# A two-layer transformer/state-space kernel: the stage ahead of the scan rebuilt, expert pieces given new places

## The chip, the cores and the metric

The kernel runs on one core of a Trainium2 chip. The core has a matrix engine (PE, with its weight loads shown as PEld), a vector engine (DVE), a scalar engine for activations (ACT), GpSimd (POOL) and a queue engine (SP) that issues most transfers. The metric is the device time of one launch in microseconds (us), median of three runs.

## What is computed

Eight sequences (B = 8) of T = 512 tokens with 128 features pass through two layers. Each layer norm is modulated by a conditioning vector, and each block is gated before it is added to the residual.

```python
# layer 0
x = x + g0 * attention(mod(layernorm(x)))          # 8 heads, latent keys and values, causal softmax
gates = top2_softmax(h @ w_gate.T)                 # 8 experts of 64 hidden units, computed densely
x = x + g1 * sum_e gates[:, e] * (gelu(h @ fc_e) @ proj_e)
# layer 1
x_in, res = split(h @ in_proj_w + b)               # 256 + 256 channels
xc = silu(conv4(x_in) + conv_b)                    # causal, 4 taps
d_raw, Bm, Cm = split(xc @ x_proj_w + b)
delta = softplus(d_raw @ dt_proj_w + dt_proj_b)
for n in range(16):                                # state index; a scan over the 512 tokens
    h[n, t] = exp(delta * A[n]) * h[n, t-1] + delta * xc * Bm[n]
y = sum_n h[n] * Cm[n] + xc * D_skip
x = x + g2 * ((y * silu(res)) @ out_proj_w + b)
x = x + g3 * top2_moe(mod(layernorm(x)))           # 8 experts of 512 hidden units, top 2 of 8
```

The experts of layer 1 are computed sparsely: tokens are sorted by expert into 15 blocks of 128 rows (`NB = 15`), each with the weights of one expert (512 KB).

## The kernel before

**One sequence after another, software-pipelined.** Each engine has a program written out by hand, in order, and engines meet only at semaphores. An iteration `b` goes through four stages: attention of `b` (DVE `attend`, L1542 on); the stage ahead of the scan (layer 0's experts, then in-projection, convolution, x-projection and softplus); the scan; then attention of `b+1` begins. Into this order the layer-1 experts of sequence `b-1` are laid ("behind"), and the projections of `b+1` ("ahead"): `project(b+1, k)` on PE and `take_queries`, `take_keys`, `take_values` on ACT.

**The scan.** There are 16 states and 2 halves of the channels, so 32 scan instructions, k = 2n + c. For each k, ACT makes the decay `exp(delta * A[n])` in one of three PSUM banks (`decays(k)`, L1242), which may begin when scan k-3 is done. DVE scans (L1686), and after the first scan of state n it multiplies state n-1 by C (`read_product`, L1351). So DVE's order is scan 2n, read n-1, scan 2n+1. PE's step n (`scan`, L1027) waits for read n-1 (`rd_ok`), then makes C of state n (L1036), sums read n-1 (L844), and then does the expert pieces that a table gives for n. POOL makes the injected term three states ahead.

**The expert pieces.** `FILLS` is a list of fills: "quad" fills transpose four blocks of tokens (ACT then writes `slots_T`), "block" fills are the first matrix product of a block (ACT then applies Gelu into `hidden`). `results(n)` is a block's second product. `PE_EARLY` and `ACT_EARLY` give the pieces laid into the stage ahead of the scan (`early(k)`), `PE_SCAN[n]` those after PE's step n, and `ACT_SCAN[k]` those that ACT does after `decays(k)` and before `decays(k+1)`. When an `ACT_SCAN` entry holds a block fill, ACT loads the Gelu table, does the Gelus, and loads the exp table back (L1253, L1256). Weights of a block are fetched by SP into one of `WR` buffers (`fetch_expert`, L460); `SP_EXPERTS` says at which point.

**Ahead of the scan.** DVE picks the two experts (`choose`), makes gates (`weigh`), widens them to 512 columns (L1435), multiplies (L1634), adds the result to x (L1636), normalises (`ln_normalise`, tiles at L1399), convolves (L1652, L1656), splits the projection in three bf16 parts (L1662 to L1669), and makes `delta` and `u`. PE transposes the normalised tiles (L744) once all four are there.

## Time and profile before

| | us |
|---|---|
| median of 3 runs | 1343.49 (1338.4 to 1347.0) |
| the profiled execution | 1336.96 |
| its span, first to last instruction | 1335.2 |
| PE busy | 1027.3 (77%) |
| DVE busy | 1010.8 (76%) |
| ACT busy | 756.4 (57%) |
| POOL busy | 628.4 (47%) |
| mean granted clock of PE | 0.898 |

No engine is busy all the time; the stages take turns. Eight times in the span the same pattern of stages comes back. Within a stage one reads which engine runs without gaps, and where it does not, what released it.

### The profile page before, as it was taken

What the parts mean: (1) busy time and instruction counts of PE and PEld (TensorE: products, weight loads), DVE (VectorE), ACT (ScalarE), POOL (GpSimd) and SP (SyncE); (2) the same over time, 40 slices, a digit from 0 to 9 for tenths busy, and PEclk for the clock granted to TensorE, in tenths of its full rate; (3) what the DMA queues carried; (4) which work ended last, traced back from release to release, by engine and by line L of the source; (5) the groups of instructions that cost most, each with busy time, mean ns of one, the idle gap of its engine ahead of it and who ended that gap; (6) DMA issues with size and microseconds to landing.
All of it is one profiled execution on the core that took longest, in us unless ns stands there. A gap on an engine that the chain in (4) does not pass through costs nothing. (4 is left out here: it accounts for less than half of the span.)

```text
span 1335.2 us, 19661 instructions
## 1 busy us (share of the span) xinstructions
PE 1027.3 (77%) x6224; PEld 702.7 (53%) x6224; DVE 1010.8 (76%) x2221; ACT 756.4 (57%) x1499; POOL 628.4 (47%) x438
## 2 busy tenths in 40 slices
PE   6875688958986888958986888958986887957291
PEld 4541145645654555646654555646654555645181
DVE  3766977689877988689877988689877987689301
ACT  3535355576646775576646775576646774476030
POOL 1004932088324953188324953187324952088402
PEclk9996579979997999979997999979997999979596
DMA  5102103252134413252134413252134413152351
GB/s 161 73 17 79 48 8 110 74 187 80 43 113 160 165 39 109 86 183 79 46 110 162 163 38 110 88 182 79 45 111 161 164 31 109 67 186 86 119 190 50
DMA packets 74151, 137.24 MB, mean 103 GB/s; under 512 B 10504, under 2 KB 44344, under 8 KB 73920
## 3 DMA queue, kind: packets, MB, share of 16 engines
q1 hardware_dynamic: 67936, 123.20, 28.2%
q0 software_dynamic: 5392, 12.59, 3.0%
q8 instruction: 51, 0.84, 0.2%
q14 instruction: 52, 0.43, 0.1%
q10 hardware_dynamic: 720, 0.19, 0.1%
HBM read 116.34 MB, written 15.42 MB: 99 GB/s over the span
## 5 line engine op out<-in xcount | busy, mean ns | idle before, releaser
L1686 DVE TENSOR_TENSOR_SCAN probs_T<-bank,probs_T 128x512 f32<-128x512 f32 x256 | 299.9, 1206 | 18.3 <-POOL probs_T L598 8.6
L598 POOL TENSOR_TENSOR probs_T<-step_space,probs_T 128x1024 f32<-128x1024 f32 x120 | 281.6, 2355 | 6.4 <-DVE probs_T L1686 6.4
L1246 ACT ACTIVATE bank<-step_space,a_neg 128x512 f32<-128x512 f32 x256 | 167.6, 683 | 76.3 <-DVE probs_T L1686 63.1
L1176 ACT ACTIVATE probs<-bank,row_neg 128x128 f32<-128x128 f32 (+3 forms) x256 | 135.0, 529 | 125.2 <-DVE row_neg L1553 107.8
L880 PE MATMUL bank<-k_pad,q_lat 128*128 128x512 f32 (+3 forms) x512 | 184.9, 447 | 2.6 <-DMA k_pad<-xc 2.6
L1553 DVE TENSOR_REDUCE row_neg<-bank 128x1 f32<-128x128 f32 (+3 forms) x256 | 122.5, 485 | 76.3 <-PE bank L882 74.2
L1036 PE MATMUL bank<-split,select 96*128 96x512 bf16 x128 | 54.7, 427 | 157.1 <-DVE probs L1351 138.2
L844 PE MATMUL bank<-probs,w_ident 128*128 128x512 f32 x256 | 158.0, 703 | 8.1 <-DVE probs L1351 8.1
L617 POOL TENSOR_TENSOR step_space<-step_space,probs 128x512 f32<-128x512 f32 x112 | 142.1, 1268 | 44.9 <-DVE probs L1351 44.6
L1351 DVE TENSOR_TENSOR probs<-probs_T,bank 128x1024 f32<-128x1024 f32 x128 | 153.1, 1196 | 9.3 <-PE bank L1036 8.9
L791 PEld LDWEIGHTS bank<-expert_w,hidden 128*128 128x128 f32 x960 | 132.1, 213 | 33.9 <-issue 33.1
L791 PE MATMUL bank<-expert_w,hidden 128*128 128x128 f32 x960 | 148.2, 303 | 0.0
L776 PEld LDWEIGHTS bank<-slots_T,expert_w 128*128 128x128 f32 x960 | 127.5, 193 | 16.0 <-issue 11.6
L569 POOL DMA_INDIRECT slots_dram<-xn_slots,slot x64 | 63.1, 986 | 154.7 <-issue 154.7
L776 PE MATMUL bank<-slots_T,expert_w 128*128 128x128 f32 x960 | 127.7, 276 | 0.0
L890 PE MATMUL bank<-w_ident,probs 128*128 128x128 f32 x640 | 113.2, 279 | 13.6 <-DVE probs_T L1562 12.8
L1036 PEld LDWEIGHTS bank<-split,select 96*128 96x128 bf16 x128 | 12.5, 98 | 205.5 <-DVE probs L1351 184.6
L890 PEld LDWEIGHTS bank<-w_ident,probs 128*128 128x128 f32 x640 | 69.9, 142 | 65.0 <-issue 36.8
L581 POOL DMA_INDIRECT rows<-results_dram,slot x64 | 61.6, 963 | 90.1 <-DMA results_dram<-slots_out 49.9
L1089 ACT ACTIVATE hidden<-bank 128x512 f32<-128x512 f32 x120 | 68.6, 596 | 54.4 <-PE bank L776 54.0
L596 POOL TENSOR_TENSOR probs_T<-step_space,probs_T 128x512 f32<-128x512 f32 x16 | 23.2, 1449 | 134.4 <-DVE step_space L1675 134.4
L880 PEld LDWEIGHTS bank<-k_pad,q_lat 128*128 128x128 f32 x512 | 81.3, 198 | 8.4 <-issue 7.9
(217 smaller groups left out, 1835.9 us busy)
## 6 DMA issues: line engine op xcount, KB each, us to landing
expert_w<-in_experts_dram SPq DMA_DIRECT2D x120, 512.0 KB, 4.1
probs_T<-b_rows_dram SPq DMA_DIRECT2D x64, 512.0 KB, 4.0
...
```

The source lines that it names most:

```text
L598: ins = nc.gpsimd.tensor_tensor(inject[:, n % 3, :, :], u[:], row.unsqueeze(1).to_broadcast([P, DH, T]), ALU.mult)
L617: ins = nc.gpsimd.tensor_tensor(state_sum[:, 1, :], state_sum[:, 1, :], read[:, n % 2, 1, :], ALU.add)
L776: ins = mm(to[:, c * P:(c + 1) * P], expert_w[:, n % WR, c * P:(c + 1) * P], slots_T[:, n // QUAD % 2, i * P:(i + 1) * P], start=False, st ...
L791: ins = mm(to[:, i * P:(i + 1) * P], hidden[:, n % HR, c * P:(c + 1) * P], expert_w[:, n % WR, F1 + c * P:F1 + (c + 1) * P], start=False, ...
L844: mm(bank[SUM_BANK][:], ident[:], read[:, n % 2, 0, :], start=(n == 0), stop=(n == NS - 1)).then_inc(sum_mm.sem, 1)
L880: mm(s[:, 0:(i + 1) * P], q_lat[:, g, i * P:(i + 1) * P], k_pad[:, g, j, 0:(i + 1) * P], start=True, stop=False)
L890: ins = tr(bank[4 + n % 2][:, k * P:(k + 1) * P], probs_ring[:, n % 4, k * P:(k + 1) * P], ident[:])
L1176: f(probs_ring[:, n % 4, 0:(i + 1) * P], bank[SCORE_BANK[n % 4]][:, 0:(i + 1) * P], ACT.Exp, bias=row_neg[:, n % 4:n % 4 + 1], accum_out=r ...
L1246: f(decay(k)[:], delta[:, c, :], ACT.Exp, scale=a_neg[:, c, n:n + 1]).then_inc(dec_ok.sem, 1)
L1351: tt(read[:, n % 2, :, :], state[:, n % 2, :, :], bank[C_BANK][:].unsqueeze(1).to_broadcast([P, DH, T]), ALU.mult).then_inc(rd_ok.sem, 1)
L1553: v.reduce_max(row_neg[:, n % 4:n % 4 + 1], bank[SCORE_BANK[n % 4]][:, 0:(i + 1) * P], AX_X, negate=True).then_inc(s_max.sem, 1)
L1686: v.tensor_tensor_scan(state[:, n % 2, c, :], decay(DH * n + c)[:], inject[:, n % 3, c, :], 0.0, ALU.mult, ALU.add).then_inc(st_ok.sem, 1)
```

## The change

- **Gates and tiles chunk by chunk.** The widened gates are written in four instructions of 512 columns with a signal each (`gates_ok` counts `C0` = 4), and PE turns each chunk as it comes. Normalised tiles signal one by one (`normed`), and PE transposes each as it comes. The copy of the logits is gone (they are read from PSUM), the gate formula is three small instructions after tanh's wait or before it where there were five.
- **Softplus of a clipped input.** Was max(z, 0) + ln(1 + exp(-|z|)), now max(z, ln(1 + exp(min(z, 20)))). DVE clips (`clip_dt`), ACT does Exp and Ln chunk by chunk; ACT's Abs is gone.
- **New order.** The convolution goes by `CONV_ORDER`; ACT's in-projection outputs, conv outputs, keys and values of `b+1` change places; `project(b+1, 3)` and `(b+1, 4)` move behind the transposes; `combine` of `b-2` comes in three parts.
- **Experts.** Six weight buffers (`WR`) instead of four, paid for by shared memory (`y_T` is `slots_T`, `hT[3]` is `hT[2]`, `bias_rest` lies in `hidden`); other lists of fills; `early` has three places on PE (two on ACT) where it had six (four). Fewer pieces are early, and the tables of pieces in the scan are new. One bank (6) holds the results of all quads.

```diff
-WR = 4
+WR = 6
@@ PE, main
+                    pe.wait_ge(*normed(b, j, t + 1))          # in layernorm, ahead of each tile
-                    if ahead and c == 2:
-                        project(b + 1, 3)
 ...
                 ins.then_inc(out0_mm.sem, 1)
-                if ahead:
-                    project(b + 1, 4)
-                if behind and ahead:
-                    pe.wait_ge(v_out.sem, v_out.at(b + 1, 1))
                 early(0)
                 layernorm(b, 2, MISC, (gates_ok.sem, gates_ok.at(b, 1)))
-                early(1)
+                if ahead:
+                    project(b + 1, 3)
                 h_wait(b, 2)
                 for c in range(2 * DH):
                     if c == 2:
-                        early(2)
+                        early(1)
+                        if ahead:
+                            project(b + 1, 4)
 ...
-                early(3)
 ...
-                early(4)
 ...
-                early(5)
+                if behind:
+                    pe.wait_ge(out0_add.sem, out0_add.at(b, 1))
+                early(2)
@@ ACT, iteration
+                take_in(0)
+                take_in(1)
+                early(1)
+                nc.scalar.preload_act_table_set("silu_and_others")
+                if ahead:
+                    take_values(b + 1)
+                take_in(2)
                 if ahead:
                     act.wait_ge(k_out.sem, k_out.at(b + 1, 16 * G * HG))
+                take_conv(0)
+                take_conv(1)
+                take_in(3)
                 act.wait_ge(pr_mm.sem, pr_mm.at(b, 1))
                 f(proj[:], bank[MISC][0:PR, :], ACT.Identity, bias=w["x_proj_b"][:]).then_inc(pr_out.sem, 1)
+                nc.scalar.preload_act_table_set("natural_log_exp_and_others")
                 for c in range(DH):
-                    mark(f(dt_abs[:, c, :], bank[HID0_BANK[c]][:], ACT.Abs, bias=w["dt_b"][:, c:c + 1]))
+                    act.wait_ge(dt_z.sem, dt_z.at(b, c + 1))
+                    mark(f(dt_exp[:, c, :], dt_low[:, c, :], ACT.Exp))
                     act.wait_ge(chain_a.sem, chain_a.at(b, c + 1))
                     f(dt_log[:, c, :], dt_exp[:, c, :], ACT.Ln, bias=1.0).then_inc(dt_l.sem, 1)
@@ DVE
+                for c in range(C0):
+                    two = slice(c * E // C0, (c + 1) * E // C0)
+                    ts(gates_wide[:, :, two, :], gates0[:, :, two].unsqueeze(3).to_broadcast([P, NT, E // C0, F0]),
+                       0.5, None, ALU.mult).then_inc(gates_ok.sem, 1)
 ...
+                clip_dt(0)
                 link(tt(part[low, :], proj[low, :], split[low, :], ALU.subtract))
+                clip_dt(1)
+                link(cp(split[low, :], part[low, :]))
                 for c in range(DH):
                     dve.wait_ge(dt_l.sem, dt_l.at(b, c + 1))
+                    stt(delta[:, c, :], bank[HID0_BANK[c]][:], w["dt_b"][:, c:c + 1], dt_log[:, c, :], ALU.add, ALU.max
+                        ).then_inc(delta_ok.sem, 1)
                     dve.wait_ge(delta_ok.sem, delta_ok.at(b, c + 1))
                     tt(u[:, c, :], delta[:, c, :], xc[:, c, :], ALU.mult).then_inc(u_ok.sem, 1)
+                tt(split[low, :], part[low, :], split[low, :], ALU.subtract).then_inc(split_ok.sem, 1)
@@ tables
+CONV_ORDER = ((0, 0), (0, 1), (1, 0), (2, 0), (1, 1), (3, 0), (2, 1), (3, 1))
-FILLS = [("quad", 0)]
+FILLS = [("quad", 0), ("quad", 1)]
 for _n in range(NB):
     FILLS.append(("block", _n))
-    if _n % QUAD == 1 and _n // QUAD + 1 < NQ:
+    if _n % QUAD == 0 and 0 < _n // QUAD < NQ - 1:
         FILLS.append(("quad", _n // QUAD + 1))
-PE_EARLY = (_fills(0, 4) + _done(0),
+PE_EARLY = (_fills(0, 4),
             _fills(4, 5),
-            _done(1) + _fills(5, 6),
-            _done(2) + _fills(6, 7),
-            _done(3),
-            _fills(7, 8))
-PE_SCAN = {1: _done(4) + _fills(8, 9) + _done(5), 2: _fills(9, 11),
-           4: _done(6) + _fills(11, 12), 5: _done(7) + _fills(12, 13),
-           7: _done(8) + _fills(13, 14), 8: _done(9) + _fills(14, 15), 9: _fills(15, 16),
-           10: _done(10), 11: _fills(16, 17) + _done(11), 12: _fills(17, 18),
-           13: _done(12) + _fills(18, 19), 14: _done(13), 15: _done(14)}
-ACT_EARLY = (_fills(0, 4), _fills(4, 5), _fills(5, 6), [("results", 0)])
-ACT_SCAN = {2: _fills(6, 8), 6: _fills(8, 9), 8: _fills(9, 11), 14: _fills(11, 13), 15: [("results", 1)],
-            18: _fills(13, 14), 22: _fills(14, 16), 26: [("results", 2)], 28: _fills(16, 18), 31: _fills(18, 19)}
+            _done(0) + _fills(5, 6) + _done(1) + _fills(6, 7))
+PE_SCAN = {1: _done(2) + _fills(7, 8), 2: _done(3) + _fills(8, 9), 3: _fills(9, 10),
+           4: _done(4), 5: _done(5) + _fills(10, 11), 6: _fills(11, 12) + _done(6), 7: _done(7) + _fills(12, 13),
+           8: _fills(13, 15), 9: _done(8), 10: _done(9) + _fills(15, 16), 11: _done(10) + _fills(16, 17),
+           12: _done(11) + _fills(17, 18), 13: _fills(18, 19), 14: _done(12), 15: _done(13, 14)}
+ACT_EARLY = (_fills(0, 4), _fills(4, 5))
+ACT_SCAN = {2: _fills(5, 7), 4: _fills(7, 8), 6: [("results", 0)], 8: _fills(8, 10), 12: _fills(10, 12),
+            14: _fills(12, 13), 16: [("results", 1)], 18: _fills(13, 15), 22: _fills(15, 17), 25: [("results", 2)],
+            28: _fills(17, 19)}
-SP_EXPERTS = {"head": (4, 5, 6), 1: (7,), 5: (8, 9), 6: (10,), 7: (11,), "end": (12, 13, 14)}
-SP_SAVES = {2: (0,)}
+SP_EXPERTS = {3: (6,), 4: (7, 8), 5: (9,), 6: (10, 11), 7: (12,), "end": (13, 14)}
+SP_SAVES = {6: (0,)}
```

The new list of fills, by number: 0 quad 0, 1 quad 1, 2 to 6 blocks 0 to 4, 7 quad 2, 8 to 11 blocks 5 to 8, 12 quad 3, 13 to 18 blocks 9 to 14. The old one: 0 quad 0, 1 and 2 blocks 0 and 1, 3 quad 1, 4 to 7 blocks 2 to 5, 8 quad 2, 9 to 12 blocks 6 to 9, 13 quad 3, 14 to 18 blocks 10 to 14.

## Rows read from the trace of the kernel before

**Rows 1.** Windows view: busy us of each engine, granted PE clock, DMA.

```profile
core 0: us, PE busy (x) PEld busy (x) DVE busy (x) ACT busy (x) POOL busy (x), PEclk, DMA share, GB/s
530.90:571.90 41.00, 33.73 (x199) 24.20 (x199) 30.00 (x72) 21.78 (x35) 7.90 (x6) 0.98 0.35 108
...
571.90:628.70 56.80, 43.21 (x223) 30.50 (x224) 53.08 (x47) 42.79 (x57) 53.04 (x30) 0.86 0.38 133
```

**Rows 2.** One line's instructions, L1435: durations, first and last start.

```profile
L1435 DVE COPY probs<-gates x8: 1226/1226/1227, 86.1 to 1138.8; 128x2048 f32<-128x2048 f32 x8
```

**Rows 3.** Timeline of DVE in one scan: start, us, instructions [idle before, releaser].

```profile
571.87 1.22 DVE L1686 TENSOR_TENSOR_SCAN probs_T<-bank,probs_T 128x512 f32<-128x512 f32 x1
...
584.84 1.22 DVE L1351 TENSOR_TENSOR probs<-probs_T,bank 128x1024 f32<-128x1024 f32 x1 [1.32 <-PE bank L1036]
...
590.56 2.34 DVE L1686 TENSOR_TENSOR_SCAN probs_T<-bank,probs_T 128x512 f32<-128x512 f32 x2 [1.14 <-ACT bank L1246]
...
627.53 1.21 DVE L1686 TENSOR_TENSOR_SCAN probs_T<-bank,probs_T 128x512 f32<-128x512 f32 x1
630.24 0.62 DVE L1553 TENSOR_REDUCE row_neg<-bank 128x1 f32<-128x128 f32 x2 [1.50 <-PE bank L882]
```

**Rows 4.** Timeline of ACT in the same scan.

```profile
583.10 0.78 ACT L1084 ACTIVATE slots_T<-bank,mod 128x512 f32<-128x512 f32 x1 [3.33 <-PE bank L765]
...
585.09 1.28 ACT L1253 ACT_TABLE_LOAD   x1
...
587.92 0.60 ACT L1089 ACTIVATE hidden<-bank 128x512 f32<-128x512 f32 x1 [0.51 <-PE bank L776]
588.54 1.28 ACT L1256 ACT_TABLE_LOAD   x1
589.84 2.67 ACT L1246 ACTIVATE bank<-step_space,a_neg 128x512 f32<-128x512 f32 x4
```

**Rows 5.** Timeline of PE in the same scan.

```profile
577.97 0.61 PE L1036 MATMUL bank<-split,select 96*128 96x512 bf16 x1 [8.73 <-DVE probs L1351]
578.37 1.91 PE L844 MATMUL bank<-probs,w_ident 128*128 128x512 f32 x2
...
582.00 1.06 PE L765 MATMUL bank<-w_ident,slots_in 128*128 128x128 f32 x4
...
584.64 1.02 PE L844 MATMUL bank<-probs,w_ident 128*128 128x512 f32 x2
...
586.83 1.05 PE L776 MATMUL bank<-slots_T,expert_w 128*128 128x128 f32 x8
...
590.63 1.11 PE L791 MATMUL bank<-expert_w,hidden 128*128 128x128 f32 x8
```

**Rows 6.** Windows view of three stretches of that scan.

```profile
578.00:584.00 6.00, 6.00 (x22) 4.63 (x23) 5.52 (x5) 1.59 (x3) 6.00 (x4) 0.50 0.30 100
598.00:601.00 3.00, 0.89 (x3) 0.21 (x2) 3.00 (x4) 2.97 (x5) 3.00 (x2) 1.00 0.48 175
601.00:604.50 3.50, 3.50 (x12) 2.27 (x11) 3.50 (x4) 1.59 (x3) 3.50 (x3) 0.52 0.39 152
```

**Rows 7.** Timeline of DVE ahead of that scan.

```profile
537.27 1.23 DVE L1435 COPY probs<-gates 128x2048 f32<-128x2048 f32 x1
...
544.81 0.69 DVE L1636 TENSOR_TENSOR x<-x,bank 128x512 f32<-128x512 f32 x1 [1.76 <-PE bank L983]
...
548.65 1.12 DVE L1399 TENSOR_SCALAR xn<-x,meanvar,rstd 128x128 f32<-128x128 f32 x4
...
555.57 0.55 DVE L1652 TENSOR_SCALAR probs_T<-xi,w_conv_w,w_conv_b 128x512 f32<-128x512 f32 x1 [0.31 <-ACT xi L1222]
556.03 4.06 DVE L1656 SCALAR_TENSOR_TENSOR probs_T<-xi,w_conv_w,probs_T 128x512 f32<-128x512 f32 x6
```

**Rows 8.** Timeline of PE ahead of that scan.

```profile
551.36 0.60 PE L744 MATMUL bank<-w_ident,xn 128*128 128x128 f32 x4
```

**Rows 9.** Timeline of ACT ahead of that scan.

```profile
562.72 0.69 ACT L1230 ACTIVATE proj<-bank,w_x_proj_b 112x512 f32<-112x512 f32 x1 [0.24 <-PE bank L1017]
```

More of the change, by code:

```diff
@@ L114, in build @@
         hidden = sb("hidden", [P, HR, T])
+        bias_rest = hidden[0:96, 0, 0:2 * P]
         slots_out = sb("slots_out", [P, 2, QUAD * P])
@@ L147, in build @@
         xn_slots = sb("xn_slots", [P, NT, P])
-        hT = [sb(f"hT{j}", [P, T]) for j in range(4)]
+        hT = [sb(f"hT{j}", [P, T]) for j in range(3)]
+        hT.append(hT[2])
         q_lat = sb("q_lat", [P, G, T])
@@ L160, in build @@
         inv_T = sb("inv_T", [P, 2 * P])
-        y_T = sb("y_T", [P, G, T])
-        logits = sb("logits", [P, NT, E])
+        y_T = slots_T
         r_a = sb("r_a", [P, NT, E])
@@ L210, in build @@
         part = mix_space[0:3 * BC, 14 * T:15 * T]
-        dt_exp, dt_abs, dt_log = conv[0], conv[1], within(8, DH)
+        dt_exp, dt_low, dt_log = conv[0], conv[1], within(8, DH)
         xc = sb("xc", [P, DH, T])
@@ L216, in build @@
         split = sb("split", [3 * BC, T], BF16)
-        dt_in, delta, u = (step_space[:, k, :, :] for k in range(3))
-        state_sum, y_skip, z = dt_in, delta, u
+        state_sum, delta, u = (step_space[:, k, :, :] for k in range(3))
+        y_skip, z = delta, u
         bank = [ctx.enter_context(nc.psum_tensor(f"bank{i}", [P, T], F32)) for i in range(8)]
-        C_BANK, HID0_BANK, GATE_BANK, OUT_BANK, MISC = 1, (4, 5), (0, 4, 5, 0), 6, 7
+        C_BANK, HID0_BANK, GATE_BANK, OUT_BANK, MISC = 1, (4, 5), (0, 2, 3, 0), 6, 7
         SUM_BANK = 7
@@ L398, in nth, with normed @@
             return of(pair, j), pair[j > 0].at(b, max(j, 1))
+        def normed(b, j, tiles=NT):
+            return of(ln_xn, j), ln_xn[j > 0].at(b, (max(j, 1) - 1) * NT + tiles)
         def linker(eng, sig, b):
@@ L483, in spread_rows @@
             def spread_rows(b, behind):
-                if behind:
-                    for n in SP_EXPERTS["head"]:
-                        fetch_expert(b - 1, n)
                 sp.wait_ge(pr_out.sem, pr_out.at(b, 1))
@@ L783, in results @@
                 q, i = divmod(n, QUAD)
-                to = bank[TAIL_BANK[q] if tail else SLOT_BANK[q]]
+                to = bank[TAIL_BANK[q] if tail else SLOT_BANK]
                 pe.wait_ge(fill_out.sem, fill_out.at(b, block_at(n)))
-                if i == 0 and q >= 2 and not tail:
+                if i == 0 and q >= 1 and not tail:
                     pe.wait_ge(slots_done.sem, slots_done.at(b, q))
@@ L1097, in take_results @@
                     act.wait_ge(saved[q % 2].sem, saved[q % 2].at(b, 16 * (q // 2)))
-                f_(slots_out[:, q % 2, 0:n * P], bank[TAIL_BANK[q] if tail else SLOT_BANK[q]][:, 0:n * P], ACT.Copy
+                f_(slots_out[:, q % 2, 0:n * P], bank[TAIL_BANK[q] if tail else SLOT_BANK][:, 0:n * P], ACT.Copy
                    ).then_inc(slots_done.sem, 1)
@@ L1204, in iteration, with take_in @@
                     take_keys(b + 1, 0)
-                route(b, 0)
                 for c in range(C0):
+                    if c == 1:
+                        route(b, 0)
                     act.wait_ge(hid0_mm.sem, hid0_mm.at(b, c + 1))
                     f(hid0[:, c, :], bank[HID0_BANK[c % 2]][:], ACT.Gelu).then_inc(hid0_act.sem, 1)
+                early(0)
+                ln_modulate(b, 2, MISC)
                 if ahead:
                     take_keys(b + 1, 1)
-                if ahead:
-                    take_values(b + 1)
-                early(0)
-                ln_modulate(b, 2, MISC)
-                early(1)
-                for c in range(2 * DH):
-                    if c == DH:
-                        early(2)
-                        nc.scalar.preload_act_table_set("silu_and_others")
+                def take_in(c):
                     act.wait_ge(in_mm.sem, in_mm.at(b, c + 1))
@@ L1418, in choose @@
                     if k == 0:
-                        link(stt(r_b[:], pick, FAR, logits[:], ALU.mult, ALU.add))
+                        link(stt(r_b[:], pick, FAR, logits, ALU.mult, ALU.add))
             def weigh(b, layer, mark, link):
                 wide = [P, NT, E]
+                if layer == 0:
+                    mark(tt(r_a[:], pick2, pick1, ALU.subtract))
+                    link(tt(r_b[:], pick1, pick2, ALU.add))
                 dve.wait_ge(gap_out.sem, gap_out.at(b, layer + 1))
@@ L1712, in _ @@
                 expert_head(B - 1, k, head)
-            for k in range(2):
+            for k in range(3):
                 combine(B - 2, k)
@@ L1730, in _ @@
                    ).then_inc(last_half, 1)
-CHAIN = {"tail": 2, "attend": 15, "main": 32, "head": 20, "act main": 4}
+CHAIN = {"tail": 2, "attend": 15, "main": 30, "head": 19, "act main": 2}
+CONV_ORDER = ((0, 0), (0, 1), (1, 0), (2, 0), (1, 1), (3, 0), (2, 1), (3, 1))
+TAPS = [at for at in CONV_ORDER if at[0] < 3]
 NORM_STEPS = 12
```

120 lines of the change are left out of this document (50 added, 70 removed).

## The prediction

> **What bounds the kernel now.** I read the page first (no engine is busy throughout), then one line that comes once per sequence: L1435 runs 8 times from 86.1 to 1138.8, so a sequence takes 150.4 us [rows 2]. Then the windows view of one sequence, stage by stage. The reader is to see two different limits. In the scan DVE is busy 53.08 of 56.80 us [rows 1]: it is the bound, with 3.7 us of gaps. Ahead of the scan nobody is full (DVE 30.0, PE 33.7 of 41 us) [rows 1]: that stage is a chain from engine to engine. The remaining 52.6 us are attention, which the change leaves alone.
>
> Then the timeline of the scan, engine by engine. From scan 9 at 590.56 to scan 31 at 627.53 lie 11 states, so a state without a gap takes 3.36 us [rows 3], that is three DVE instructions of 1.12. The reader should note what the two visible gaps are: 1.32 waiting for PE's C, and 1.14 waiting for ACT's decay 9 [rows 3]. The second is a law of this kernel in small. ACT did decay 8, loaded the Gelu table at 585.09, waited twice for PE's fills, did the second Gelu at 587.92, loaded the exp table back at 588.54, and only then decay 9, from 589.84, ready at 590.53 [rows 4]: DVE's scan 9 starts at 590.56. So a decay that stands behind a Gelu trip is ready 0.60 + 1.28 + 0.69, with the gaps 2.6 us, after PE's last fill of that trip. The old tables pay this once; in their other trips the fills lie ahead of the trip.
>
> **The change: expert pieces in the scan (a loss).** PE's step n cannot begin before read n-1 is done, and ACT's piece after decay k stands in front of decay k+1. Both rules stay; only the tables change. I walk each new ACT entry: in which PE step is its last fill, when is it ready, and when is decay k+1 due. PE's prices at full clock, as distances from start to start in these rows: C 0.22, sum 0.87, a block fill 1.11, results 1.01, a quad 0.5 (half of 1.06, which ran at half clock) [rows 5]. Time zero is the end of the read that releases the PE step; 0.1 is for the last matmul's end.
>
> - k=4, quad 2, in step 1 (behind results 2): ready at 0.22+0.87+1.01+0.5+0.1 = 2.7; ACT writes it in 0.78, decay 5 takes 0.69: 4.2. Decay 5 is due one state later, 3.36. Stall 0.8.
> - k=8, blocks 5 and 6, the second in step 3: 2.3, plus 2.6: 4.95. Decay 9 due at 3.36. Stall 1.6.
> - k=12, blocks 7 and 8, the second in step 6. Read 5, which releases step 6, comes after scan 12, and scan 13 follows it at once: decay 13 is due at 0 and comes at 4.95, with handovers 5.05. Stall 5.05.
> - k=14, quad 3, in step 7 behind results 7: decay 15 is due at 0, ready at 2.7 + 0.7 + 0.7. Stall 4.1.
> - k=18, blocks 9 and 10, both in step 8: 0.22+0.87+2.22+0.1 = 3.4, plus 2.65; due at 3.36. Stall 2.7.
> - k=22, block 12 in step 11 behind results 10: 3.3 plus 2.65, due at 0. Stall 5.95.
> - k=25, results of quad 2, complete in step 12: 2.1 + 0.65 + 0.7, due after one scan, 1.12. Stall 2.35.
> - k=28, block 14 in step 13: 2.3 plus 2.6, due at 3.36. Stall 1.55.
>
> The entries k=2, 6 and 16 find their pieces done. The old tables stand the other way round: the fills for k=14 are in steps 4 and 5, for k=22 in steps 8 and 9, so each is ready a scan or two before ACT comes. The stalls add up, since each is counted from a read that is itself later: 24.1 us per sequence at full clock.
>
> **The clock.** PE went idle before 577.97 for 8.73 us, and ran at half clock from 578 to 584: the sum took 1.91 instead of 1.02 [rows 5, 6]. Even after 598 to 601, with PE busy 0.89 of 3, the granted clock was 0.52 in the next stretch [rows 6]. The new stalls make longer waits than that one: PE ends step 6 at 3.4 and gets step 7 at 5.05+3.36 = 8.4, so 5 us idle; the same before step 8 (4.1 + 3.36 against 2.6) and before step 12 (5.95 + 3.36 against 3.3: 6 us); before step 1 it is idle some 5.5 us. I take these four steps at half clock for most of their PE part: +2.6 (k=4), +2.2 (k=14), +2.2 (k=18), +2.1 (k=25), 9.1 in all. For the others I take full clock. Bounds: only step 1 slow, +2.6; every step slow, +20.3.
>
> On this the Trainium skill has a rule (TensorE: Matmul & The Clock Gate, section on HAM oscillation): a loop whose burst of matmuls is followed by a longer wait is throttled again each round, and every burst starts cold. The two rows above agree as far as they go; by the rule alone the last bound would hold.
>
> The Trainium skill also prices a table switch (ScalarE: Activation LUTs, "What ACT_TABLE_LOAD costs") at 1283 ns plus a drain of 1380 ns. In this trace the load takes 1.28 and the decay starts 0.02 after it [rows 4], so I take no drain. By the page, decay k+1 would come 1.38 later in each of the five stalling Gelu trips (k=8, 12, 18, 22, 28): 6.9 us per sequence more, 1580 in all.
>
> **The change: ahead of the scan (a gain).** Four steps, each against this sequence's rows.
>
> - Tiles of the first norm one by one, no copy of logits, shorter gate formula: about 0.4 + 0.2 = 0.6 us earlier at the gates.
> - Gates in four chunks cost 4 x 0.46 (L1652's start to the next, also a tensor_scalar of 512 columns) instead of 1.23 [rows 7], but PE turns the first while DVE writes the rest, and only one chunk instead of two is turned behind the first product: 0.6 earlier at L1636. Together x is added at 543.65 instead of 544.81 [rows 7].
> - The second norm's tiles were ready at 549.77 [rows 7], but PE began them at 551.36 [rows 8], behind expert pieces and a projection. Now less stands before them (two quads, two fills, from 543.5 to 547.3), so tiles go as they come: last one at 549.0, against 551.96. That is 3.0 in all.
> - Convolution: DVE waits for the two inputs and then runs 6 taps in 4.06 [rows 7]. The new order ends half 0 at 555.9 and half 1 at 557.3, so ACT's silu, the x-projection and ACT's `proj` end at 559.8 instead of 563.41 [rows 9]: 3.6 in all. The keys' DMAs of b+1 now start 11 us later and land about 555, just ahead of this; if they were later, ACT's first silu would wait for them.
> - From `proj` to the first scan it is 8.46 us now (563.41 to 571.87) [rows 3, 9]. Abs leaves ACT, but the table load moves behind `proj`, clips go to DVE, and the last split moves between `u` and the first scan. DVE has as many instructions there as before, and POOL's first injections follow the second `u` as before. I take 0, with bounds of -1.5 (the second chunk's Exp and Ln overlap) and +1 (DVE's `u` held up by POOL).
>
> The gain is 3.6 us per sequence (2 to 5). It is on the path, as the stage is a chain. In sequence 0, with no experts behind, I take 2.
>
> **The end of the scan.** Step 15 now holds two results instead of one, and the scores of the next attention stand behind them. DVE already waits 1.50 there for PE [rows 3], so 1.0 more is lost per sequence.
>
> **Six buffers.** No gap in the rows of this scan is released by a transfer [rows 3 to 5], so this is worth nothing there; it covers fetches made later, and in the tail it is worth about 1 us.
>
> **Sum.** Gaps in the scan: 24.1 + 9.1 + 1.2 at the start (the present gaps less the two of rows 3, 3.7 - 1.32 - 1.14; they are waits for POOL's first injections) = 34.4 against 3.7 now: +30.7. With -3.6 and +1.0: +28.1 per sequence, for the seven that carry experts (1 to 7): +197. Less 2 and 1: +194. The profiled execution took 1336.96, so 1531. The median of the runs is 6.5 above that execution; I predict 1532.
>
> **Rivals.**
>
> - A, the forecast: four steps at half clock. 1532. Chance 0.52.
> - B, the same stalls, but PE's clock recovers quickly in steps 7, 8 and 12: 6.5 less per sequence, 1485; with no slow step at all 1467. For it: in this trace the clock came back after 6 us of full work [rows 6]. Chance 0.26.
> - C, the skill's loop as a mechanism here: every stall cools PE for the next step, each PE part doubles, +20.3 instead of +9.1 per sequence: 1609. Against it: most steps carry over 2 us of work in 3.36, and steps like that ran at full clock after 584 [rows 5]. Chance 0.10.
> - D, the other side: the trips are hidden, because decay banks or PE run further ahead than I read. Then only -3.6 + 1.0 per sequence is left: 1337 - 18 - 3 = 1316. Its place is k=12, 14 and 22; it decides once the stalls add under 2.6 us to the present gaps, instead of 30.7. Against it: scan 9's row, where the law shows to 0.03 us [rows 3, 4]. Chance 0.07.
> - E, the chain ahead of the scan does not shorten (the keys' DMAs or POOL's port take the gain): 1556. Chance 0.05.
>
> **Numbers.** This kernel's measurement can tell about 1% from no change. The range takes A with B and E, from 1467 to 1575 (A with the slower side of its clock, 6 us per sequence more). Faster by over 1%: D, 0.06; within 1%: 0.02; slower: 0.92.
>
> **What would show it.** In the profile after: ahead of the scans, DVE idle released by ACT's decays some 200 us in all, where this sequence has one gap of 1.14 [rows 3]; the longest before scans 13, 15, 19 and 23; ACT's Gelu and `slots_T` waiting for PE 2 to 5 us in the trips after decays 12, 14 and 22; a scan stage of some 87 us instead of 56.9; the clock at 0.5 after each long wait. The gain shows in L744's second run, in `proj` coming 3.6 us earlier after the attention. The prediction is wrong if the scan stage stays under 62 us; off in size if stalls are there but the steps' clock is other than said.

## The result

The changed kernel takes 1557.7 us (median of 4 runs, 1556.4 to 1561.2) against 1343.5: 1.160 of the time before, 95% interval 1.156 to 1.164. Its profiled execution has a span of 1554.8 us, 219.6 more than before. The prediction was 1532, range 1467 to 1575.

The page names the place. The first row is DVE's scan, with its busy time and then the idle time ahead of it by releaser; the second is ACT's Gelu of the expert blocks.

```profile
L1690 DVE TENSOR_TENSOR_SCAN probs_T<-bank,probs_T 128x512 f32<-128x512 f32 x256 | 300.6, 1211 | 258.1 <-ACT bank L1242 249.8
...
L1080 ACT ACTIVATE hidden<-bank 128x512 f32<-128x512 f32 x120 | 70.9, 597 | 194.3 <-PE bank L775 194.0
```

DVE's scans are as busy as before, but they wait 249.8 us for ACT's decays, and ACT's Gelus wait 194.0 us for PE's fills. The windows view of one sequence (busy us of PE, PEld, DVE, ACT, POOL, granted clock, DMA) sorts it by stage: ahead of the scan, the scan, and the attention.

```profile
590.60:627.12 36.52, 31.12 (x170) 20.46 (x169) 29.57 (x73) 21.05 (x32) 8.23 (x7) 1.00 0.28 77
627.12:716.65 89.53, 52.51 (x241) 36.56 (x242) 53.61 (x47) 44.38 (x59) 52.94 (x30) 0.82 0.28 96
716.65:770.00 53.35, 48.51 (x359) 32.29 (x357) 40.23 (x151) 30.58 (x97) 17.82 (x19) 0.98 0.27 89
```

The scan stage grew from 56.8 [rows 1] to 89.5 us while DVE's work in it stayed (53.1, now 53.6). Its timeline on DVE shows each gap, the idle time and its releaser in brackets:

```profile
627.12 2.36 DVE L1690 TENSOR_TENSOR_SCAN probs_T<-bank,probs_T 128x512 f32<-128x512 f32 x2
...
638.90 2.34 DVE L1690 TENSOR_TENSOR_SCAN probs_T<-bank,probs_T 128x512 f32<-128x512 f32 x2 [2.65 <-ACT bank L1242]
...
647.44 2.34 DVE L1690 TENSOR_TENSOR_SCAN probs_T<-bank,probs_T 128x512 f32<-128x512 f32 x2 [1.73 <-ACT bank L1242]
...
660.55 2.34 DVE L1690 TENSOR_TENSOR_SCAN probs_T<-bank,probs_T 128x512 f32<-128x512 f32 x2 [6.30 <-ACT bank L1242]
...
669.61 2.34 DVE L1690 TENSOR_TENSOR_SCAN probs_T<-bank,probs_T 128x512 f32<-128x512 f32 x2 [5.61 <-ACT bank L1242]
...
681.48 2.34 DVE L1690 TENSOR_TENSOR_SCAN probs_T<-bank,probs_T 128x512 f32<-128x512 f32 x2 [5.06 <-ACT bank L1242]
...
695.65 2.34 DVE L1690 TENSOR_TENSOR_SCAN probs_T<-bank,probs_T 128x512 f32<-128x512 f32 x2 [7.36 <-ACT bank L1242]
...
704.64 1.22 DVE L1690 TENSOR_TENSOR_SCAN probs_T<-bank,probs_T 128x512 f32<-128x512 f32 x1 [4.41 <-ACT bank L1242]
...
712.07 2.34 DVE L1690 TENSOR_TENSOR_SCAN probs_T<-bank,probs_T 128x512 f32<-128x512 f32 x2 [1.73 <-ACT bank L1242]
...
720.64 0.62 DVE L1552 TENSOR_REDUCE row_neg<-bank 128x1 f32<-128x128 f32 x2 [4.00 <-PE bank L881]
```

These are the gaps before scans 5, 9, 13, 15, 19, 23, 26 and 29, 34.9 us together, and the wait for the first scores. ACT's timeline around the largest early one is the same picture as [rows 4], drawn out:

```profile
649.40 1.28 ACT L1248 ACT_TABLE_LOAD   x1
655.73 0.60 ACT L1080 ACTIVATE hidden<-bank 128x512 f32<-128x512 f32 x1 [5.05 <-PE bank L775]
657.92 0.60 ACT L1080 ACTIVATE hidden<-bank 128x512 f32<-128x512 f32 x1 [1.59 <-PE bank L775]
658.53 1.28 ACT L1251 ACT_TABLE_LOAD   x1
659.83 1.30 ACT L1242 ACTIVATE bank<-step_space,a_neg 128x512 f32<-128x512 f32 x2
```

The table was loaded, ACT stood 5.05 us, did a Gelu, stood 1.59 more, and decay 13 came at last at 660.5: scan 13 starts at 660.55.

### The profile page after: what moved, and what is told of

Same layout as the page of the kernel before. It is cut to its first block and busy times, and to the rows that moved or that the text cites. A ratio compares the mean times of both kernels' runs of the same rounds, so it can differ in the third digit from the quotient of the medians.

```text
span 1554.8 us, 19644 instructions
## 1 busy us (share of the span) xinstructions
PE 1101.2 (71%) x6224; PEld 739.7 (48%) x6224; DVE 1009.9 (65%) x2221; ACT 761.7 (49%) x1490; POOL 630.1 (41%) x438
## 5 line engine op out<-in xcount | busy, mean ns | idle before, releaser
L1690 DVE TENSOR_TENSOR_SCAN probs_T<-bank,probs_T 128x512 f32<-128x512 f32 x256 | 300.6, 1211 | 258.1 <-ACT bank L1242 249.8
L1027 PE MATMUL bank<-split,select 96*128 96x512 bf16 x128 | 63.8, 499 | 297.1 <-DVE probs L1346 278.5
L843 PE MATMUL bank<-probs,w_ident 128*128 128x512 f32 x256 | 188.0, 827 | 8.6 <-DVE probs L1346 8.6
L1080 ACT ACTIVATE hidden<-bank 128x512 f32<-128x512 f32 x120 | 70.9, 597 | 194.3 <-PE bank L775 194.0
L790 PEld LDWEIGHTS bank<-expert_w,hidden 128*128 128x128 f32 x960 | 144.7, 231 | 43.9 <-issue 43.4
L790 PE MATMUL bank<-expert_w,hidden 128*128 128x128 f32 x960 | 159.7, 320 | 0.0
L775 PEld LDWEIGHTS bank<-slots_T,expert_w 128*128 128x128 f32 x960 | 142.5, 213 | 20.7 <-issue 14.2
L775 PE MATMUL bank<-slots_T,expert_w 128*128 128x128 f32 x960 | 140.2, 294 | 0.0
L1075 ACT ACTIVATE slots_T<-bank,mod 128x512 f32<-128x512 f32 (+1 forms) x32 | 23.2, 748 | 159.3 <-PE bank L764 159.2
L889 PEld LDWEIGHTS bank<-w_ident,probs 128*128 128x128 f32 x640 | 69.9, 142 | 63.4 <-issue 34.9
```

The source lines that it names most:

```text
L775: ins = mm(to[:, c * P:(c + 1) * P], expert_w[:, n % WR, c * P:(c + 1) * P], slots_T[:, n // QUAD % 2, i * P:(i + 1) * P], start=False, st ...
L790: ins = mm(to[:, i * P:(i + 1) * P], hidden[:, n % HR, c * P:(c + 1) * P], expert_w[:, n % WR, F1 + c * P:F1 + (c + 1) * P], start=False, ...
L843: mm(bank[SUM_BANK][:], ident[:], read[:, n % 2, 0, :], start=(n == 0), stop=(n == NS - 1)).then_inc(sum_mm.sem, 1)
L889: ins = tr(bank[4 + n % 2][:, k * P:(k + 1) * P], probs_ring[:, n % 4, k * P:(k + 1) * P], ident[:])
L1690: v.tensor_tensor_scan(state[:, n % 2, c, :], decay(DH * n + c)[:], inject[:, n % 3, c, :], 0.0, ALU.mult, ALU.add).then_inc(st_ok.sem, 1)
```

## The experiments

All are timed against the kernel before.

**ACT's table alone.** PE's table, the rebuilt stage and the buffers stay.

```diff
-ACT_SCAN = {2: _fills(5, 7), 4: _fills(7, 8), 6: [("results", 0)], 8: _fills(8, 10), 12: _fills(10, 12),
-            14: _fills(12, 13), 16: [("results", 1)], 18: _fills(13, 15), 22: _fills(15, 17), 25: [("results", 2)],
-            28: _fills(17, 19)}
+ACT_SCAN = {2: _fills(5, 7), 6: _fills(7, 8), 7: [("results", 0)], 10: _fills(8, 10), 16: _fills(10, 12),
+            18: _fills(12, 13), 19: [("results", 1)], 22: _fills(13, 15), 26: _fills(15, 17), 28: [("results", 2)],
+            31: _fills(17, 19)}
```

> The changed kernel with one table edited: ACT's pieces come later among the decays (quad 2 after decay 6, blocks 5 and 6 after 10, 7 and 8 after 16, quad 3 after 18, 9 and 10 after 22, 11 and 12 after 26, 13 and 14 after 31), so that each fill is complete on PE a state or more before decay k+1 is due. PE's table, the stage ahead of the scan and the six buffers stay. Theory (the decays stand behind Gelu trips that wait for PE): the gaps before scans 13, 15, 19, 23, 26 and 29 vanish, 30 us per sequence; about 1318, 1.5 to 2.5% faster than the kernel before, with the gain ahead of the scan kept. Rival (the cost sits in the rebuilt stage, the memory sharing, the single results bank or the buffers): over 1450.

Measured: 1298.48 us, ratio 0.968 (0.963 to 0.972). One table gives back 259 us and turns the loss into a gain. The scan's row in the groups view, and the scan stage in the windows view:

```profile
L1690 DVE TENSOR_TENSOR_SCAN probs_T<-bank,probs_T 128x512 f32<-128x512 f32 x256 | 299.3, 1205 | 10.9 <-POOL probs_T L597 8.6 <-ACT bank L1242 1.5
```

```profile
520.85:558.43 37.58, 31.70 (x172) 20.86 (x172) 30.62 (x76) 21.15 (x33) 8.21 (x7) 1.00 0.28 80
558.43:613.70 55.27, 44.36 (x242) 31.43 (x243) 53.09 (x47) 42.81 (x58) 52.76 (x30) 0.91 0.45 155
```

The waits for ACT are 1.5 us in the whole span instead of 249.8. The rival that blames the rebuilt stage, the shared memory or the buffers falls. The expectation was too cautious by 20 us. Against the kernel before, the stage ahead of the scan is 4.45 us shorter here too (more than I had taken, see below), and the scans got shorter as well: in the seven sequences with experts they take 54.4 to 55.3 us against 56.7 to 56.9, since the two gaps of [rows 3] are gone. In this sequence, the longest, a wait of 0.80 for ACT and one of 0.31 for POOL are left. Only the wait for the first scores is 1.0 longer.

**Both tables.** Fills a step or two earlier on PE too, ACT's trips after decays 2, 8, 14, 20, 26, 31.

```diff
 ...
+PE_SCAN = {1: _done(2) + _fills(7, 8) + _done(3), 2: _fills(8, 10), 3: _done(4), 4: _done(5) + _fills(10, 11),
+           5: _done(6) + _fills(11, 12), 6: _fills(12, 13), 7: _done(7) + _fills(13, 14), 8: _fills(14, 15),
+           9: _done(8) + _fills(15, 16), 10: _done(9) + _fills(16, 17), 11: _done(10), 12: _done(11) + _fills(17, 18),
+           13: _fills(18, 19) + _done(12), 14: _done(13), 15: _done(14)}
 ...
```

> The changed kernel with both tables of pieces edited: PE does each fill a step or two earlier than ACT's trip needs it (trips after decays 2, 8, 14, 20, 26, 31), one results piece in step 15 instead of two. Theory: as act_late, and the second results piece no longer delays the first scores, 1 to 2.5 us per sequence more: about 1305. Rival (the single results bank or the fewer early pieces cost time by themselves): 1345 or more.

Measured: 1303.42 us, ratio 0.972 (0.966 to 0.977), as expected in size but not better than the first. Its timeline on DVE has the two gaps of the kernel before in it again [rows 3]:

```profile
570.69 1.22 DVE L1346 TENSOR_TENSOR probs<-probs_T,bank 128x1024 f32<-128x1024 f32 x1 [1.26 <-PE bank L1027]
...
576.41 2.34 DVE L1690 TENSOR_TENSOR_SCAN probs_T<-bank,probs_T 128x512 f32<-128x512 f32 x2 [1.14 <-ACT bank L1242]
```

Step 1, at half clock, holds three pieces in it and makes C late; the trip after decay 8 costs 1.14. The 1.0 us that it wins at the end of the scan it loses there.

**The clock.** The changed kernel, with matmuls nobody reads in PE's waits.

```diff
+                    if behind and n in WARM:
+                        f, times = WARM[n]
+                        pe.wait_ge(fill_out.sem, fill_out.at(b - 1, f - 1))
+                        for _ in range(times):
+                            mm(fill_bank(f)[:], w["wfcT"][:, 0:P], w["in_w"][:], start=True, stop=True)
                     if n >= 1:
                         pe.wait_ge(rd_ok.sem, rd_ok.at(b, n))
+WARM = {1: (7, 4), 5: (10, 2), 7: (12, 4), 8: (13, 4), 10: (15, 3), 12: (17, 5), 15: (20, 2)}
```

> The changed kernel with 24 matmuls of 128x512 per sequence that nobody reads, laid into PE's waits ahead of steps 1, 5, 7, 8, 10, 12 and 15 (4, 2, 4, 4, 3, 5 and 2 of them, some 0.87 us each, into a fill bank that the next fill overwrites). Theory (a wait of 3 us and more costs the next step half its clock): these seven steps run at full clock; decays 5, 13, 15, 19, 23, 26 and the first scores come 1.2 to 2.4 us earlier each, 12 us per sequence; about 1474, with the gaps before scans 13, 15, 19, 23 at 5.1, 4.1, 2.7 and 6.0. Rival (the slow steps do not matter, or the clock falls anyway): 1558 or more.

Measured: 1487.26 us, ratio 1.109 (1.103 to 1.114): 70 us less than the changed kernel for doing more work. Three gaps on DVE in one sequence, before scans 5, 9 and 13:

```profile
619.78 2.34 DVE L1695 TENSOR_TENSOR_SCAN probs_T<-bank,probs_T 128x512 f32<-128x512 f32 x2 [0.82 <-ACT bank L1247]
...
628.32 2.34 DVE L1695 TENSOR_TENSOR_SCAN probs_T<-bank,probs_T 128x512 f32<-128x512 f32 x2 [1.73 <-ACT bank L1247]
...
640.22 2.34 DVE L1695 TENSOR_TENSOR_SCAN probs_T<-bank,probs_T 128x512 f32<-128x512 f32 x2 [5.09 <-ACT bank L1247]
```

These are the prediction's full-clock figures, 0.8, 1.6 and 5.05; those after them, 3.96, 2.84, 6.09 and 2.43, are 4.1, 2.7, 5.95 and 2.35. So the split of each stall into a part that the order makes and a part that the clock adds is shown. 70 us instead of 84 because the clock was not kept everywhere: in this sequence it fell within step 13 (its fill took 1.83 instead of 1.05), and the gap before scan 29 was 2.51 instead of 1.55. This is one of the better sequences: with 80.2 us for its scans it lies in a range of 79.4 to 83.0, and in four of six sequences the wait for the first scores stood at 4.0 to 4.2 us again, where it is 2.50 in this one.

**The law in the old kernel.** The kernel before, one entry moved.

```diff
-ACT_SCAN = {2: _fills(6, 8), 6: _fills(8, 9), 8: _fills(9, 11), 14: _fills(11, 13), 15: [("results", 1)],
+ACT_SCAN = {2: _fills(6, 8), 6: _fills(8, 9), 8: _fills(9, 11), 12: _fills(11, 13), 15: [("results", 1)],
```

> The kernel before with one entry moved: the Gelus of blocks 8 and 9 after decay 12 instead of 14; PE's steps 4 and 5 as they are. Theory (decay k+1 comes 2.65 us after the last fill's end): block 9's fill ends 3.3 us after read 4, so decay 13 is ready at 5.95 where it is due at 3.36: a gap of 2.6 us before scan 13 in each of seven sequences, about 1361. Rival (the two early trips have slack and hide it): 1343, no gap.

Measured: 1354.0 us, ratio 1.011 (1.006 to 1.017). The gap stands before scan 13:

```profile
757.05 2.34 DVE L1686 TENSOR_TENSOR_SCAN probs_T<-bank,probs_T 128x512 f32<-128x512 f32 x2 [2.73 <-ACT bank L1246]
```

The scans' row of the page:

```profile
L1686 DVE TENSOR_TENSOR_SCAN probs_T<-bank,probs_T 128x512 f32<-128x512 f32 x256 | 299.9, 1207 | 36.7 <-ACT bank L1246 26.3 <-POOL probs_T L598 8.6 <-POOL probs_T L596 1.5
```

In the whole span the scans' wait for ACT is 26.3 us, 18.3 more than the 8.0 of before: 7 times 2.6. The times say somewhat less: 17 us between the two profiled spans, 14 between medians.

**The end of the scan.** The kernel of the first experiment with one results piece moved to step 14.

```diff
-           12: _done(11) + _fills(17, 18), 13: _fills(18, 19), 14: _done(12), 15: _done(13, 14)}
+           12: _done(11) + _fills(17, 18), 13: _fills(18, 19), 14: _done(12, 13), 15: _done(14)}
```

> act_late with one results piece moved from PE's step 15 to step 14. Theory (the scores of the next attention stand behind step 15's pieces): the wait of DVE before the first row maximum falls from 2.50 to 1.5 us in each of seven sequences; about 1291, 0.963 of the kernel before. Rival (the piece waits in step 14 for its Gelu after decay 31 and delays C of state 15): 1298 or more, with a gap before the last read.

Measured: 1294.2 us, ratio 0.964 (0.960 to 0.969), the fastest of all here by its profile (span 1290.7 against 1298.8). The first row maximum, in this kernel and then in the first experiment's:

```profile
611.63 0.62 DVE L1552 TENSOR_REDUCE row_neg<-bank 128x1 f32<-128x128 f32 x2 [1.50 <-PE bank L881]
```

```profile
616.20 0.62 DVE L1552 TENSOR_REDUCE row_neg<-bank 128x1 f32<-128x128 f32 x2 [2.50 <-PE bank L881]
```

One piece is 1.0 us, as expected, but six times and not seven: behind the last sequence's scan no attention follows. Between the two kernels' times alone the difference (4 us) is within their uncertainty.

**Parts of the rebuilt stage.** Each is the first experiment's kernel with one part set back. What counts is where DVE is, from the start of the first norm's tiles.

```diff
-CONV_ORDER = ((0, 0), (0, 1), (1, 0), (2, 0), (1, 1), (3, 0), (2, 1), (3, 1))
+CONV_ORDER = ((0, 0), (0, 1), (1, 0), (1, 1), (2, 0), (2, 1), (3, 0), (3, 1))
```

> act_late with the taps in the old order, both halves alternating. The x-projection needs both halves; the new order ends half 0 about 1.4 us earlier, but half 1 about 0.25 us later for two waits on itself. Theory A (the new order is what brings proj forward): some 1 us per sequence slower, 1306. Theory B (the last half sets the end, and the first half's silu and product only move into the wait): within 0.3 us per sequence, 1296 to 1301.

Measured: 1299.56 us, ratio 0.967 (0.963 to 0.971), no difference that the time can tell. In the trace the bf16 split of `proj` starts 29.75 us after the tiles instead of 29.47: 0.28 per sequence. ACT's two silus and `proj`, in the old order and then the new:

```profile
545.71 1.15 ACT L1213 ACTIVATE xc<-probs_T 128x512 f32<-128x512 f32 x2 [0.97 <-DVE probs_T L1656]
548.40 0.69 ACT L1228 ACTIVATE proj<-bank,w_x_proj_b 112x512 f32<-112x512 f32 x1 [0.97 <-PE bank L1010]
```

```profile
546.65 0.63 ACT L1213 ACTIVATE xc<-probs_T 128x512 f32<-128x512 f32 x1 [0.44 <-DVE probs_T L1656]
547.77 0.63 ACT L1213 ACTIVATE xc<-probs_T 128x512 f32<-128x512 f32 x1 [0.48 <-DVE probs_T L1656]
549.60 0.69 ACT L1228 ACTIVATE proj<-bank,w_x_proj_b 112x512 f32<-112x512 f32 x1 [0.63 <-PE bank L1010]
```

The first half is early, but `proj` waits for the second. Theory B holds.

```diff
-                for c in range(C0):
-                    two = slice(c * E // C0, (c + 1) * E // C0)
-                    ts(gates_wide[:, :, two, :], gates0[:, :, two].unsqueeze(3).to_broadcast([P, NT, E // C0, F0]),
-                       0.5, None, ALU.mult).then_inc(gates_ok.sem, 1)
+                ts(gates_wide[:], gates0[:].unsqueeze(3).to_broadcast([P, NT, E, F0]), 0.5, None, ALU.mult
+                   ).then_inc(gates_ok.sem, 4)
```

> act_late with the widened gates written by one instruction instead of four. Theory: PE's first turn comes some 1 us later and so does all behind it, less what DVE saves; the sum into x comes 0.7 us later per sequence, 1304. Rival: DVE's multiplications hide it, no change.

Measured: 1303.94 us, ratio 0.970 (0.966 to 0.974). Against 0.968 the time can't tell it; the trace can. The gates and the sum into x, written in four and then in one:

```profile
527.62 1.43 DVE L1433 TENSOR_SCALAR probs<-gates 128x512 f32<-128x512 f32 x4
...
534.02 0.69 DVE L1637 TENSOR_TENSOR x<-x,bank 128x512 f32<-128x512 f32 x1 [1.32 <-PE bank L980]
```

```profile
529.82 1.23 DVE L1431 TENSOR_SCALAR probs<-gates 128x2048 f32<-128x2048 f32 x1
...
536.92 0.69 DVE L1635 TENSOR_TENSOR x<-x,bank 128x512 f32<-128x512 f32 x1 [1.32 <-PE bank L980]
```

From gates to sum 6.40 against 7.10: 0.7 per sequence, as expected, although the four instructions take 0.2 us longer than the one.

```diff
-                    mark(f(dt_exp[:, c, :], dt_low[:, c, :], ACT.Exp))
-                    act.wait_ge(chain_a.sem, chain_a.at(b, c + 1))
+                    mark(f(dt_low[:, c, :], bank[HID0_BANK[c]][:], ACT.Abs, bias=w["dt_b"][:, c:c + 1]))
+                for c in range(DH):
+                    act.wait_ge(chain_a.sem, chain_a.at(b, c + 1))
+                    mark(f(dt_exp[:, c, :], dt_low[:, c, :], ACT.Exp, scale=-1.0))
+                for c in range(DH):
+                    act.wait_ge(chain_a.sem, chain_a.at(b, DH + c + 1))
 ...
-                    stt(delta[:, c, :], bank[HID0_BANK[c]][:], w["dt_b"][:, c:c + 1], dt_log[:, c, :], ALU.add, ALU.max
-                        ).then_inc(delta_ok.sem, 1)
+                    stt(delta[:, c, :], state_sum[:, c, :], 0.0, dt_log[:, c, :], ALU.max, ALU.add
+                        ).then_inc(delta_ok.sem, 1)
```

> act_late with the softplus of before (Abs, Exp, Ln on ACT, each for both halves; the sum with the bias on DVE after ACT's Abs). Theory (the prediction's zero for this part): from proj to the first scan stays within 0.5 us of now (8.15 us), 1296 to 1303. Rival (the clipped form is where the gain of the rebuilt stage comes from): 2 us per sequence or more, over 1312.

Measured: 1303.98 us, ratio 0.971 (0.966 to 0.975). From the split to the first scan it is 8.87 us (552.95 to 561.82) against 8.11 with the clipped form: 0.76 per sequence, more than the half microsecond of the theory and well under the 2 of the rival. It comes in two halves. The first `delta` begins 4.38 us after the split instead of 3.92, since DVE waits twice (0.22 and 0.42) while ACT does its Abs, Exp and Ln. And the second `u` takes 1.64 instead of 1.21. It runs beside POOL's first injection and ends 0.55 us after it in both kernels; that injection takes 1.63 here instead of 1.26, and why is not shown.

```profile
559.38 1.64 DVE L1683 TENSOR_TENSOR step_space<-step_space,xc 128x512 f32<-128x512 f32 x1
561.05 0.68 DVE L1684 TENSOR_TENSOR split<-probs_T,split 32x512 bf16<-32x512 f32 x1
561.82 2.36 DVE L1695 TENSOR_TENSOR_SCAN probs_T<-bank,probs_T 128x512 f32<-128x512 f32 x2
```

**Four buffers.** The kernel of the end-of-scan experiment, with fetches a step later where they must be.

```diff
-WR = 6
+WR = 4
-SP_EXPERTS = {3: (6,), 4: (7, 8), 5: (9,), 6: (10, 11), 7: (12,), "end": (13, 14)}
+SP_EXPERTS = {1: (4, 5), 3: (6,), 4: (7,), 5: (8,), 6: (9, 10), 7: (11,), "end": (12, 13, 14)}
```

> The kernel best with four weight buffers instead of six; the fetches of blocks 4 and 5 go ahead of the second pair of B rows, 6 to 11 one step later each. Theory (the prediction's: six buffers are worth nothing in the scan): block 4's weights land some 4 us after results 0, just as PE would need them; the B rows for states 2 and 3 come behind two more transfers; 0 to 1 us per sequence, 1294 to 1302. Rival (the early pieces need the weights ahead): block 4's fill waits 3 us or more, and with it C of state 0 and the Gelu trip after decay 2: over 1315.

Measured: 1307.17 us, ratio 0.975 (0.970 to 0.981): about 1% slower than with six, which lies between the two expectations. On PE, on DVE and on POOL:

```profile
561.78 0.59 PE L771 MATMUL bank<-own,bias 96*128 96x512 bf16 x1 [3.05 <-issue]
```

```profile
569.91 1.22 DVE L1690 TENSOR_TENSOR_SCAN probs_T<-bank,probs_T 128x512 f32<-128x512 f32 x1 [1.28 <-POOL probs_T L597]
...
575.87 1.22 DVE L1346 TENSOR_TENSOR probs<-probs_T,bank 128x1024 f32<-128x1024 f32 x1 [1.38 <-POOL step_space L613]
```

```profile
567.47 6.98 POOL L597 TENSOR_TENSOR probs_T<-step_space,probs_T 128x1024 f32<-128x1024 f32 x3 [2.42 <-DMA probs_T<-b_rows_dram]
```

Block 4's fill stands 3.05 us (the profile names no releaser; its weights are the only thing that the program waits for there), but in this sequence DVE never waits for what stands behind it on PE. What costs time is the other transfer: the B rows come behind two weight transfers, POOL waits 2.42 for them, and DVE waits 1.28 for POOL's injected term and 1.38 for a read buffer. With six buffers the first of these gaps is absent and the second is 0.31. So the rival is right that the weights come late, and wrong about the path on which it costs.

**One fill ahead of the transposes.** Again the end-of-scan kernel.

```diff
-PE_EARLY = (_fills(0, 4),
-            _fills(4, 5),
+PE_EARLY = (_fills(0, 5),
+            [],
             _done(0) + _fills(5, 6) + _done(1) + _fills(6, 7))
-ACT_EARLY = (_fills(0, 4), _fills(4, 5))
+ACT_EARLY = (_fills(0, 5), [])
```

> The kernel best with block 2's fill ahead of the second norm's transposes, behind blocks 0 and 1, instead of between the in-projections. Theory (each piece that PE does ahead of those transposes past the arrival of the tiles delays the whole chain): PE is free at 606.3 there and the tiles are there from 606.9 to 607.7; the fill ends at 607.5, so the transposes come 0.4 us later; ACT's Gelu stands before its modulation, 0.5 to 0.9 us per sequence in all; the end of the stage is later by 0 to 0.9: 1294 to 1301. Rival (the fill between the in-projections cost as much there): no change or faster.

Measured: 1308.29 us, ratio 0.977 (0.974 to 0.981), about 14 us slower, more than expected, and for another reason. The convolution's first input comes just as late after the second norm's tiles as before (4.26 us in both). What is later is the x-projection. In this kernel, and then without the move:

```profile
549.23 3.40 PE L1010 MATMUL bank<-xc,w_x_proj_w 128*112 128x512 f32 x4 [2.52 <-ACT xc L1213]
```

```profile
544.52 2.23 PE L1010 MATMUL bank<-xc,w_x_proj_w 128*112 128x512 f32 x4 [1.41 <-ACT xc L1213]
```

The windows view of the moved kernel gives the cause:

```profile
545.00:549.00 4.00, 1.70 (x4) 0.40 (x3) 3.93 (x7) 2.54 (x4) 0.00 (x0) 0.97 0.38 111
549.00:552.60 3.60, 3.37 (x4) 1.02 (x4) 0.62 (x1) 1.38 (x3) 0.00 (x0) 0.56 0.01 2
```

With the fill gone from its place PE waits 2.52 us instead of 1.41, the granted clock falls to 0.56 (1.2 GHz for most of the stretch), and the projection takes 1.17 us longer: that is the whole delay of this sequence's stage (from the second norm's tiles to the split of `proj` 13.64 against 12.47). My theory, that the transposes would be late, was wrong: they end 1.5 us after the tiles' start in both.

It is not the cause in every sequence. In three of the other six with experts the stage's delay is about 2.5 us and stands earlier. There the x-projection came after a PE wait of 2.25 us and kept its clock, but the clock had been at half behind the first norm's tiles, after PE waits of only 0.69 and 1.03 us. The same eight matmuls of layer 0's experts take 3.81 us in the changed kernel:

```profile
381.76 5.32 PE L966 MATMUL bank<-hT,w_wfcT 128*128 128x512 f32 x8
...
405.73 1.11 PE L1010 MATMUL bank<-xc,w_x_proj_w 128*112 128x512 f32 x2 [2.25 <-ACT xc L1213]
```

In other sequences it is the other way round: full clock after the same 0.69 and 1.03 us, half clock in the x-projection after the same 2.25. So the length of the wait just before does not settle it, and what does is not shown.

## Why the prediction was right, and what was off

**Direction and mechanism: right.** The law read off one gap of 1.14 us [rows 3, 4] carried over to eight gaps and to the old kernel. By gap, in us, forecast and then measured in this sequence:

| before scan | 5 | 9 | 13 | 15 | 19 | 23 | 26 | 29 |
|---|---|---|---|---|---|---|---|---|
| forecast, full clock | 0.8 | 1.6 | 5.05 | 4.1 | 2.7 | 5.95 | 2.35 | 1.55 |
| forecast, with slow steps | 3.4 | 1.6 | 5.05 | 6.3 | 4.9 | 5.95 | 4.45 | 1.55 |
| measured | 2.65 | 1.73 | 6.30 | 5.61 | 5.06 | 7.36 | 4.41 | 1.73 |

The sum was to be 33.2 and is 34.9. That it comes so close is partly luck: two gaps were 0.7 us shorter than the forecast and two 1.3 to 1.4 longer.

**The clock: the term that was mis-sized.** The step that failed is "for the others I take full clock". I drew the line at PE waits of 5 us. In the changed kernel steps 5, 10 and 15 came after waits of 2.92, 4.09 and 2.92 us and were slow as well:

```profile
650.94 0.61 PE L1027 MATMUL bank<-split,select 96*128 96x512 bf16 x1 [2.92 <-DVE probs L1346]
651.34 1.91 PE L843 MATMUL bank<-probs,w_ident 128*128 128x512 f32 x2
```

The sum of step 5 took 1.91 instead of 1.02 [rows 5]. Step 6, which holds the fill for scan 13's trip, could begin only when step 5 was through, so the gap before scan 13 was 6.30 instead of 5.05; step 10 does the same to scan 23. [rows 6] already had a slow stretch behind one in which PE was idle only 2.1 of 3 us; I read it and then did not use it. On the other side, steps 1 and 7 had their clock back before their last piece, the quad (the gaps are 2.65 and 5.61, not 3.4 and 6.3). In all the clock was to add 9.1 us per sequence and added 12.3 here: 10.8 in the gaps (34.9 less the 24.1 at full clock) and 1.5 at the end of the scan. (Over the span DVE waited 249.8 us for the decays. The "some 200" among the signs was less than the forecast's own sum, seven times 33.2 or 232.)

**The end of the scan: off for the same reason.** Forecast 1.0 for the second results piece; measured 2.5 (4.00 against 1.50 [rows 3]). The end-of-scan experiment shows the piece itself to be 1.0; the remaining 1.5 is step 15 at half clock, where C took 0.61 and the sum 1.91. With matmuls in that wait (the clock experiment) it is gone: 2.50 in the sequence shown. The price is paid six times, not seven.

**Ahead of the scan: right in sign, too small.** The first scan starts 37.59 us after the first norm's tiles instead of 42.04, a gain of 4.45 against the 3.6 of the sum. By step, gain up to that point:

| | gates | x added | taps begin | split of proj | first scan |
|---|---|---|---|---|---|
| forecast | 0.6 | 1.2 | | 3.6 | 3.6 |
| measured | 0.67 | 1.81 | 3.62 | 4.13 | 4.45 |

The sum into x is 0.6 earlier than I worked out. From the gates to that sum 1.14 us are gained where I had 0.6. The experiment with one instruction gives 0.70 of them to the four chunks, which cost 0.34 each from start to start and not the 0.46 that I took; the other 0.44 is what PE needs to turn one chunk, since only one is now turned behind the first product. The transposes gave 1.81, as against 1.84 in the forecast (3.0 less 1.16): they now follow the tiles.

```profile
602.70 0.69 DVE L1637 TENSOR_TENSOR x<-x,bank 128x512 f32<-128x512 f32 x1 [1.32 <-PE bank L980]
...
619.00 0.42 DVE L1667 CAST split<-proj 96x512 bf16<-96x512 f32 x1 [2.58 <-ACT proj L1228]
```

The order of the taps, to which I gave 0.6 of the gain, is worth 0.28. The part from `proj` to the first scan, costed at nothing, is 0.32 shorter than in the kernel before; with the old softplus in the new place it is 0.76 longer than with the clipped one. About half of that is ACT's chunk-by-chunk Exp and Ln and half the second `u` beside POOL: the mechanisms of my two bounds, in small.

**Six buffers: wrong.** I costed them at nothing in the scan since no row of before showed a wait for a transfer. That was a reading of the old order, with its own fetch places. The new early pieces need block 4 before the first scan; with four buffers its fetch pushes back the B rows, and the kernel is about 1% slower.

**The sum.** In this sequence the scan took 32.7 more, the stage ahead 4.45 less, the wait for the scores 2.5 more: 30.7, where the forecast had 28.1. Seven times that is 215 of the 219.6 us of the two spans, but the seven are not alike. The scans with experts take 89.5 to 91.5 us. In the last sequence the stage ahead gained nothing (43.46 us against 42.98): PE stands 3.72 us before the first norm's transposes, with no projection of a next sequence to do, and goes on at half clock (the eight matmuls L966 take 6.71 instead of 3.81). The first scan of all comes 2.6 us earlier (forecast 2), and from the last scan to the end it takes 2.3 us more, where I had a gain of 1. The measured 1557.7 is also within 2 us of rival E's 1556; that is chance, as E's mechanism, a chain that does not shorten, is not in the trace.

**The two pages.** In this sequence each of the seven PE waits of 2.92 us and more inside the scan was followed by a step that began at half clock, and none of the eight steps after shorter waits (up to 1.74 us) did. The rule on the clock (the Trainium skill, TensorE: Matmul & The Clock Gate, section on HAM oscillation), by which a burst that is shorter than the wait behind it is followed by a cold one, agrees for steps 1, 5, 8 and 15. Steps 7, 10 and 12 were slow too, though PE had worked some 8 us without a gap before waits of 4.09 to 6.18. Rival C, every step doubled, did not come. For the table switch no drain is seen in this sequence's trips: after the load at 658.53 (1.28 us) the decay starts 0.02 us later. The Trainium skill (ScalarE: Activation LUTs, "What ACT_TABLE_LOAD costs") gives 1283 ns for the load, which agrees, and a drain of 1380 ns, which is not there.
